# One keep-warm matmul instead of two behind each product of a recurrent layer

## What is computed

```python
xb = jnp.einsum('bsd,ed->sbe', x, B)
def step(h, xb_t):
    h = jnp.tanh(h @ A.T + xb_t)
    y = h @ C.T
    return (h, y)
_, ys = jax.lax.scan(step, h0, xb)
out = jnp.transpose(ys, (1, 0, 2)) + x      # then a layer norm with gamma, beta
```

## Time and profile before

| What | us |
|---|---|
| median of three runs | 3563.22 |
| the profiled execution | 3561.33 |
| its span, first to last instruction | 3559.5 |
| PE busy in the span | 3403.3 |
| DVE busy | 2822.8 |
| POOL busy | 2263.3 |
| ACT busy | 2155.9 |

### The profile page before, as it was taken

One profiled execution on the slowest core, in us unless ns is written; L12 is line 12 of the kernel. 1 busy time (PEld: TensorE's weight loads), 2 busy tenths in 40 slices (PEclk: granted clock), 3 DMA queues, 4 the chain that ended last, 5 costly groups with the idle time before them and its releaser, 6 DMA issues. The chain is left out here.

```text
span 3559.5 us, 101336 instructions
## 1 busy us (share of the span) xinstructions
PE 3403.3 (96%) x42643; PEld 2170.8 (61%) x42643; DVE 2822.8 (79%) x4367; ACT 2155.9 (61%) x4211; POOL 2263.3 (64%) x1363
## 2 busy tenths in 40 slices
PE   8999699999999999999999999999999999999996
PEld 4555366666666666666666666666666666666664
DVE  3444498888888888888888888888888888888883
ACT  2222256666666666666666666666666666666664
POOL 0000267777676777777777777677677676777773
PEclk9999899999999999999999999999999999999999
DMA  2000000100000100001000001000001000000000
GB/s 70 1 1 1 4 11 11 32 11 11 11 12 13 34 11 11 8 17 34 11 8 11 11 17 31 11 11 11 8 17 35 11 11 8 11 17 13 14 11 13
DMA packets 62282, 52.54 MB, mean 15 GB/s; under 512 B 11527, under 2 KB 59397, under 8 KB 61829
## 3 DMA queue, kind: packets, MB, share of 16 engines
q1 hardware_dynamic: 61828, 46.05, 4.9%
HBM read 43.93 MB, written 2.10 MB: 13 GB/s over the span
## 5 line engine op out<-in xcount | busy, mean ns | idle before, releaser
L431 POOL TENSOR_TENSOR cosp<-cosp,rr 128x1024 f32<-128x1024 f32 x384 | 722.6, 1903 | 636.8 <-DVE rr L922 636.6
L441 POOL TENSOR_TENSOR cosp<-cosp,sinp 128x1024 f32<-128x1024 f32 x384 | 907.7, 2369 | 101.1 <-DVE sinp L901 98.0
L623 PEld LDWEIGHTS ps<-px,w_vo 128*128 128x128 f32 x6144 | 700.5, 192 | 224.3 <-DVE sh L994 219.6
L623 PE MATMUL ps<-px,w_vo 128*128 128x128 f32 x6144 | 735.7, 278 | 66.8 <-DVE sh L994 55.6
L527 PE MATMUL ps<-w_qk,xs 128*128 128x512 f32 x1536 | 749.5, 611 | 10.0 <-ACT sq L735 5.1
L735 ACT ACTIVATE sq<-ps 128x1024 f32<-128x1024 f32 x384 | 392.3, 1021 | 402.5 <-DVE sinp L901 402.5
L898 DVE TENSOR_TENSOR cosp<-ps,tab 128x1024 f32<-128x1024 f32 x384 | 469.5, 1223 | 203.2 <-PE ps L527 202.0
L907 DVE TENSOR_REDUCE ss<-sq 128x16 f32<-128x1024 f32 x384 | 455.5, 1186 | 94.9 <-ACT sq L735 94.9
L527 PEld LDWEIGHTS ps<-w_qk,xs 128*128 128x128 f32 x1536 | 263.3, 191 | 343.6 <-issue 341.7
L683 PE MATMUL ps<-pT,xtm 32*128 32x512 f32 x3072 | 458.6, 616 | 9.8 <-DVE pT L973 4.7
L901 DVE TENSOR_TENSOR sinp<-ps,tab 128x1024 f32<-128x1024 f32 x384 | 466.6, 1215 | 0.0
(11 more groups left out here) (106 smaller groups left out, 4412.5 us busy)
## 6 DMA issues: line engine op xcount, KB each, us to landing
tab<-in_tab SPq DMA_DIRECT2D x96, 128.0 KB, 2.0
qks<-in_scales SPq DMA_DIRECT2D x96, 128.0 KB, 3.2
w_qk<-in_L_ffn_Wqkv SPq DMA_DIRECT2D x12, 512.0 KB, 7.1
w_v<-in_wv_t SPq DMA_DIRECT2D x6, 512.0 KB, 8.8
w_o<-in_L_ffn_Wo SPq DMA_DIRECT2D x6, 512.0 KB, 10.3
x<-in_L_attn_x SPq DMA_DIRECT2D x16, 128.0 KB, 3.3
out<-w_v SPq DMA_DIRECT2D x16, 128.0 KB, 2.5
w<-in_L_ffn_W SPq DMA_DIRECT2D x6, 341.0 KB
```

Source lines behind the costliest of these rows:

```text
L431: eng.tensor_tensor(v, v, rr[:, B % 2, HEADS * i:HEADS * i + HEADS].unsqueeze(2).to_broadcast([P, HEADS, DH]), ALU.mult).then_inc(rot_read ...
L441: eng.tensor_tensor(cosp[:, A % 2, i, :], cosp[:, A % 2, i, :], sinp[:, i, :], ALU.add).then_inc(rot_added, 1)
L623: t = eng.matmul(S0, w_vo[:, i // HP, i % HP, :], px[:, i, :], start=i == 0, stop=i == HEADS - 1)
```

## The change

In the loop over the steps of a chunk one of the two calls of `keep_warm()` is left out. Nothing else is different; on PE 512 matmuls fewer stand in the program.

```diff
                     eng.matmul(ps[:, r, BATCH * t:BATCH * t + BATCH], abcT[:, 0, :], prev, start=False, stop=t == FW - 1,
                                skip_group_check=True).then_inc(pre_done, 1)
                     keep_warm()
-                    keep_warm()
                     if t == AT_OUTPUT and c:
                         outputs(c - 1)
```

## The result

The changed kernel takes 3663.32 us (median of four runs, 3661.86 to 3663.63), the kernel before 3563.43 beside it: ratio 1.0275, 95% interval 1.0263 to 1.0288. That is slower by 100 us. It lies inside the range, near its upper end, and it is not the forecast case (3574) but the rival "half clock throughout, or falling back soon after each rise", for which the prediction had put 3665. Times and ratios of kernels that ran several times are of their fast executions; three others, at a mean granted clock of 0.85 or less, are left out.

What follows compares the result with a forecast made beforehand. The recurrent step was taken as bound by the product-tanh chain, 0.655 us at full clock. Terms -0.2, +15.3, +0.4 and -4.5 gave +11.0 on 3561.3, so 3572.3; the median lies 1.9 above: 3574 us, range 3554 to 3664.

Steps and rivals of the forecast that it cites:

- the forecast case: Recurrent stage: first chunk at half clock, then the clock rises and holds; 3574 us, from 3562 to 3591, chance 0.38.
- half clock throughout, or falling back soon after each rise: Recurrent stage: clock low for most of it; 3628 to 3700 us, taken as 3665, chance 0.31.
- Full-clock steps cost nothing: Ordinary steps at full clock: chain-bound at 0.655 us, so removing one filler costs and gains nothing, 1 us either way.
- the 21 places: At t = 3, 38 and 54, other PE work precedes the next product: 0.215 us saved each, 4.5 us gained.
- The stage begins at half clock and doesn't rise at 22 us: Chunk 0: steps now have PE gaps, so it runs at half clock; 60 steps at +0.255, +15.3 us.
- The half-clock step: One changed step at half clock: 0.91 us, lower bound 0.72, against 0.655 at full clock.
- The clock rises at the first dense place behind chunk 0: Chunk 1: clock rises at L505 or at L483 four steps later; 16 us more if a second chunk is needed.
- And then holds: Stage after the rise in chunk 1: clock stays at full level with one filler a step, so ordinary steps cost nothing.
- The rival's price of 3700: Whole stage at half clock: 509 steps at +0.255, +130; transposes and L483 +12; -4.5 at t = 3, 38, 54.
- the places with other work: Transposes and L483 at half clock throughout: 14 x 0.4 + 7 x 0.85 = +12 us, against -4.5 for fewer fillers.
- two cases: Recurrent stage: half the steps at half clock, 3628 us, or all of them, about 3700; 3665 was taken.

## Why the prediction came out as it did

- *Full-clock steps cost nothing:* right. In the islands of the changed kernel the tanhs are 0.655 apart with one filler, and at the 21 places the gain has the predicted size. The reason given was right (the chain), the picture beside it wrong: PE was not on the same moment but 0.085 ahead.
- *The stage begins at half clock and doesn't rise at 22 us:* right. Chunk 0, from its first tanh to its last, takes 19.71 to 74.82, 55.1 us instead of 43.0.
- *The half-clock step:* mis-sized. I took 0.91, between 0.72 and 0.91; it is 0.86. The term is the time from the first weight load to the second: 0.17, where I had 0.21 from L476's loads, which were probably paced by their matmuls. First chunk: +12.1 us, not +15.5.
- *The clock rises at the first dense place behind chunk 0:* right, to the place. Right behind the work at t = 3 of chunk 1 the tanhs turn from 0.86 to 0.65 apart, as these lines from the timelines of PE and ACT of the changed kernel show. All seven rises in its stage come within two steps of a chunk's L505 or L483.

```profile
79.97 0.18 ACT L713 ACTIVATE cosp<-ps 128x8 f32<-128x8 f32 x1 [0.68 <-PE ps L510]
80.17 1.92 PE L483 MATMUL ps<-qT,px 128*128 128x128 f32 x8
...
82.35 0.18 ACT L713 ACTIVATE cosp<-ps 128x8 f32<-128x8 f32 x1 [2.20 <-PE ps L510]
83.21 0.18 ACT L713 ACTIVATE cosp<-ps 128x8 f32<-128x8 f32 x1 [0.68 <-PE ps L510]
...
83.68 0.38 PE L494 MATMUL ps<-ident_bf 128*128 128x512 bf16 x1
83.86 0.18 ACT L713 ACTIVATE cosp<-ps 128x8 f32<-128x8 f32 x1 [0.48 <-PE ps L510]
84.09 0.39 PE L510 MATMUL ps<-cosp,qT 128*128 128x8 f32 x2
...
86.48 0.18 ACT L713 ACTIVATE cosp<-ps 128x8 f32<-128x8 f32 x1 [0.48 <-PE ps L510]
87.25 0.18 ACT L713 ACTIVATE cosp<-ps 128x8 f32<-128x8 f32 x1 [0.59 <-PE ps L510]
```

- *"And then holds":* this is the step that failed. Five steps later the clock is down (0.50 from 87 us), and so it goes in every later chunk, where it stays up for four to ten steps. I had called undecided on it, one stretch with 1.09 us of work ahead of a fall and one without a fall, and took the second. The runs decide: with one filler a step the clock falls (two kernels), with a quarter more it stays.
- The rival's price of 3700 for all steps at half clock was too high by the half-clock step: 509 x 0.205 = 104 instead of 130. The 43 steps in the islands (9 us) are most of the rest; the places with other work came out near its sum, 10.0 us with the boundaries against 12 - 4.5 = 7.5. That 3665 was so near is luck: I had taken it between two cases. It is luck too that the range held 3663: its upper end, 3664, cut this case in half.

The Trainium skill ("TensorE: Matmul & The Clock Gate", section "A second HAM failure mode: psum-queue depth-cycling") says that short, frequent pauses between groups of matmuls can make the clock swing between its levels. The trace agrees in part. In an island the filler that starts at 83.68 takes 0.215, and the next product starts at 84.09, so PE pauses for some 0.2 us of each 0.655, and the clock goes up and down through the stage; but it spends most of the stage at the lower level. Against drops in the middle of a kernel the same page of the Trainium skill, section "Why this matters for your kernels", warns of long pauses alone; by that the clock would have held, and the measurement (0.50 from 87 us) speaks against it.

## What to carry to other kernels

A filler that hides wholly under a chain is not free to remove if it also holds the clock: ask for each stretch what PE does without it, at both levels, before counting its busy time as waste. Where the clock's answer isn't in the trace, price the half-clock step from the rows that show one and give the case its full chance; here it was worth 100 us against 4.5. And test fillers by width, since a quarter or a half of one had already changed the course.

## What was not expected of the hardware

A weight load that waits for its matmul's data stands in the chain: when a filler made PE late (three of them), the load slipped under it and 0.085 us of each step were hidden. At half clock a float32 weight load is followed by the next after 0.17 us instead of 0.11; the chain of 0.655 grows to 0.86 by this and by the longer way from the load to the tanh (0.46 instead of 0.32). And the clock that twelve fillers, started at 9.1 us, had raised (1.00 from 13 to 16 us) was down again at 16.5 us, ahead of the first product, so that these fillers were lost.
